# A decoder block with routed experts: stage borders without GpSimd's drain, routing's last rounds a step ahead, expert rows and weights waited for apart, and bfloat16 pad and rank matrices

## The chip, the cores and the metric

The kernel runs on one core of one Trainium2 chip. The time is that of the device for one execution, in microseconds (us). Engines: TensorE (PE, matrix products; PEld is its weight load), VectorE (DVE), ScalarE (ACT), GpSimd (POOL), and SyncE (SP), which issues transfers.

## What is computed

The input x has 16 items of 256 tokens by 256 channels, in float32. Two decoder layers follow each other; these are the reference's last lines, with the routed experts' core:

```python
x = x + _L0_attn_ref(_layernorm(x), ...)      # 16 heads, |i - j| <= 32
x = x + _L0_xattn_ref(ctx, ctx, _layernorm(x), mask_BxS2, ...)   # 77 keys, padded
x = x + _L0_ffn_ref(_layernorm(x), ...)       # 8 experts, top 2
x = x + _L1_attn_ref(_layernorm(x), ...)      # causal
x = x + _L1_xattn_ref(_layernorm(x), ctx, ctx, mask_SxS2, ...)
x = x + _L1_ffn_ref(_layernorm(x), ...)       # gated, 4 bit weights, quantised

# _L0_ffn_ref
gate_weights = softmax(x @ gate_w + gate_b)
topk_vals, topk_idx = top_k(gate_weights, 2)
h = gelu(x @ w1[e] + b1[e]); h = gelu(h @ w2[e] + b2[e])
expert_out = h @ w3[e] + b3[e]
sum(topk_vals * take_along_axis(expert_out, topk_idx))
```

## The kernel before

The program runs in four parts, each an `nc.Block` in which every engine has its own instruction stream and the engines meet by semaphores: stage 1 of attention (window, then cross with padding, and at its end the routing of layer 0's experts), the experts, stage 2 of attention (causal, then cross with a mask), and the quantised last network. x stays in on-chip memory.

`attention()` serves both stages. It is a software pipeline over N = 32 units (16 items through self-attention, then 16 through cross-attention). `step(t, ref)` on each engine does lag 0 of unit `ref`, lag 1 of the one before and so on, in eight parts i = 0 to 7. In stage 1 lag 4 is the layer norm of the finished item, lag 5 its turning (`last_turn`, `keep_turned`), lag 6 the gate logits (`gate_logits`, `see`, `find_best`, `choose`; GpSimd's `note` keeps them), and lag 7 the ranks: `ranks` on TensorE counts with a triangular matrix `row_before`, a matrix of ones, the choices `both` and the counts `filled`, which place in its expert's region each token gets; `place` turns it into a slot; `scatter` on GpSimd casts the slots, adds to `filled`, and sends the item's rows to `slots_dram` by four indirect transfers. The last item comes to lag 7 at step N + 6. Then `tile_table` makes the table of tiles from `filled`, and SyncE writes zeros behind each expert's last row (L563), waits for them, and ends.

In the cross part `scores` adds the pad bias as a product of a selecting matrix and the padding row `pad_now` (L1301), ahead of the heads' products (L1308).

`experts()` goes over MT = 71 tiles of 128 rows, each belonging to one expert, with a ring of four buffers. SyncE loads per tile its rows (L1640, 128 KB) and the expert's packed weights (L1642, 2180 KB) when y of the tile four before is made. TensorE's order in tile j is: turn the rows of tile j + 1 (`turn_rows`, L1671), layer 2 of tile j (L1696, 32 matmuls), layer 1 of j + 1 (L1680, 16), layer 3 of j (L1706). VectorE copies the turned rows (`columns`, L1743) and adds y's bias (L1754); ScalarE does the gelus (L1724); GpSimd stores y (L1657). Aside from that, VectorE quantises the raw weights of the last network (`beside`: at tiles 0, 2, 3 and the last seven, behind the y addition), which SyncE has loaded right after tile 0 (L1648, three of 768 KB); at the end TensorE turns them in twelve runs through two PSUM buffers and ScalarE copies them out (L1737).

A part ends at its `nc.Block` line (L458 for both attention stages, L1632 for the experts, L1951 for the last network), where each engine executes a drain and then passes a barrier. Then the context manager `semaphores` clears the part's semaphores on GpSimd (L49) and has all engines pass a second barrier (L50).

## Time and profile before

| What | Value |
|---|---|
| Median of 3 runs | 2347.57 us (2342.65 to 2357.03) |
| Profiled execution | 2332.47 us, its span 2330.9 us |
| Mean granted TensorE clock | 0.949 |
| Busy share PE, DVE, ACT, POOL | 90%, 53%, 41%, 29% |
| Stage 1, experts, stage 2, last network end at | 735.5, 1294.8, 1994.9, 2330.9 us |
| Memory rate in the experts | about 341 GB/s, transfer engines over 90% busy |

All times within the program are from that one profiled execution, counted from the start of its span. A row of the timeline is: start, duration (or the busy sum of a merged group of x instructions), engine, line, operation, output<-inputs, shapes, and in brackets the idle time of the engine before it and what ended that. A q behind an engine's name means its queue: drains, waits and issues. 1.00 of the granted clock is 2.4 GHz and 0.50 is 1.2 GHz.

### The profile page before, as it was taken

How to read it: one execution, taken by the hardware profiler on the slowest of the kernel's cores; microseconds unless marked ns; L12 is line 12 of the kernel's file. 1: busy time of each engine (PE TensorE's matmuls, PEld its weight loads, DVE VectorE, ACT ScalarE, POOL GpSimd, SP SyncE). 2: the span in 40 equal slices, each digit the busy share in tenths (PEclk: the TensorE clock that was granted, in tenths of full speed). 3: DMA queues.
4: the chain of work that ended last, by engine and by line, in shares of the span. 5: the costliest groups of instructions: out<-in, count | busy, mean ns of one | idle time of the engine just before them, and what ended most of it. 6: DMA issues, size and time to landing. Idle time of an engine off the chain costs nothing. (4 is left out here: it accounts for less than half of the span.)

```text
span 2330.9 us, 50427 instructions
## 1 busy us (share of the span) xinstructions
PE 2109.1 (90%) x16962; PEld 1618.0 (69%) x16962; DVE 1228.9 (53%) x5368; ACT 962.8 (41%) x1843; POOL 675.6 (29%) x1222
## 2 busy tenths in 40 slices
PE   5999999999992999999999589999999999799869
PEld 3777777777762899999999367677766666344358
DVE  4677775555532211111113467777767776439964
ACT  1444454555541233333333235455554454237510
POOL 2555555244443000000000434544321121003410
PEclk8899999998975999999999789999999999899989
DMA  6223222222314899999996533333223222000013
GB/s 203 88 95 108 104 100 95 82 93 92 101 58 175 311 342 341 340 343 341 342 342 257 158 102 121 118 110 112 92 79 95 95 89 66 5 0 0 0 47 98
DMA packets 209352, 334.56 MB, mean 144 GB/s; under 512 B 59445, under 2 KB 193498, under 8 KB 200122
## 3 DMA queue, kind: packets, MB, share of 16 engines
q1 hardware_dynamic: 195306, 302.46, 37.1%
q0 software_dynamic: 9552, 26.10, 3.8%
q10 hardware_dynamic: 4352, 4.20, 0.5%
q8 instruction: 78, 1.28, 0.2%
q14 instruction: 64, 0.52, 0.1%
HBM read 193.72 MB, written 28.05 MB: 95 GB/s over the span
## 5 line engine op out<-in xcount | busy, mean ns | idle before, releaser
L1724 ACT ACTIVATE moe_h<-moe_h_ps,moe_weights 128x128 f32<-128x128 f32 x568 | 177.3, 363 | 368.4 <-PE moe_h_ps L1696 311.4
L1696 PE MATMUL moe_h_ps<-moe_h,moe_weights 128*128 128x128 f32 x2272 | 267.5, 276 | 0.0
L1754 DVE TENSOR_TENSOR moe_y<-moe_y_ps,moe_weights 128x256 f32<-128x256 f32 x71 | 30.2, 425 | 442.1 <-PE moe_y_ps L1706 442.1
L1696 PEld LDWEIGHTS moe_h_ps<-moe_h,moe_weights 128*128 128x128 f32 x2272 | 261.7, 193 | 0.1
L1125 ACT ACTIVATE causal_prob<-causal_ps 128x768 f32<-128x768 f32 (+1 forms) x192 | 168.6, 878 | 150.8 <-PE causal_ps L1344 149.7
L2148 PE MATMUL ffn_prod_ps<-x_sb,ffn_weights 128*128 128x512 f32 x480 | 210.5, 598 | 9.7 <-ACT ffn_sig_q L2134 7.0
L867 DVE CUSTOM_DVE_ANT_0 causal_masked<-causal_ps,causal_causal_mask 128x256 bf16<-128x256 f32 (+1 forms) x512 | 152.2, 354 | 75.4 <-PE causal_ps L1308 74.5
L1657 POOL DMA_DIRECT2D moe_y_dram<-moe_y x71 | 38.9, 547 | 519.9 <-DVE moe_y L1754 519.9
L2148 PEld LDWEIGHTS ffn_prod_ps<-x_sb,ffn_weights 128*128 128x128 f32 x480 | 90.9, 191 | 127.0 <-issue 110.0
L867 DVE CUSTOM_DVE_ANT_0 window_masked<-window_ps,window_window_mask 128x160 bf16<-128x160 f32 x512 | 135.1, 320 | 76.3 <-PE window_ps L1308 75.5
L1680 PE MATMUL moe_h_ps<-moe_rowsT,moe_weights 128*128 128x128 f32 x1136 | 140.7, 278 | 5.1 <-DVE moe_rowsT L1743 5.1
L1680 PEld LDWEIGHTS moe_h_ps<-moe_rowsT,moe_weights 128*128 128x128 f32 x1136 | 134.2, 194 | 6.3 <-DVE moe_rowsT L1743 6.3
L1706 PE MATMUL moe_y_ps<-moe_weights,moe_h 128*128 128x256 f32 x568 | 134.5, 380 | 0.7 <-ACT moe_h L1724 0.7
L1125 ACT ACTIVATE window_prob<-window_ps 128x640 f32<-128x640 f32 x128 | 89.9, 702 | 108.8 <-PE window_ps L1344 107.7
L721 POOL TENSOR_SCALAR_AFFINE_SELECT causal_prob<-causal_prob 128x512 f32<-128x512 f32 x128 | 80.2, 650 | 167.4 <-ACT causal_prob L1125 167.3
L1308 PEld LDWEIGHTS causal_ps<-k_pair,q_pair 64*128 64x128 f32 x1024 | 73.0, 188 | 67.9 <-issue 44.8
L1308 PE MATMUL window_ps<-k_pair,q_pair 64*128 64x160 f32 (+1 forms) x1024 | 96.5, 290 | 22.7 <-DVE window_m_tok L867 14.9
L1308 PEld LDWEIGHTS window_ps<-k_pair,q_pair 64*128 64x128 f32 x1024 | 78.3, 195 | 55.8 <-DVE window_m_tok L867 24.3
L1308 PE MATMUL causal_ps<-k_pair,q_pair 64*128 64x78 f32 (+2 forms) x1024 | 99.4, 296 | 19.3 <-DVE causal_m_tok L867 15.2
L2005 DVE TENSOR_REDUCE ffn_peak<-ffn_wide 128x1 f32<-128x1024 f32 x72 | 87.2, 1212 | 49.3 <-ACT ffn_wide L2108 49.3
L867 DVE CUSTOM_DVE_ANT_0 causal_masked<-causal_ps,causal_cross_mask 128x77 bf16<-128x77 f32 x512 | 86.7, 236 | 49.1 <-PE causal_ps L1308 49.1
L1706 PEld LDWEIGHTS moe_y_ps<-moe_weights,moe_h 128*128 128x128 f32 x568 | 102.5, 190 | 11.9 <-ACT moe_h L1724 0.9
(352 smaller groups left out, 4497.0 us busy)
## 6 DMA issues: line engine op xcount, KB each, us to landing
moe_weights<-moe_w_in SPq DMA_DIRECT2D x71, 2180.0 KB, 9.6
q_pair<-window_q_parts SPq DMA_DIRECT2D x256, 128.0 KB
q_pair<-causal_q_parts SPq DMA_DIRECT2D x256, 128.0 KB
k_pair<-window_k_parts SPq DMA_DIRECT2D x128, 128.0 KB
k_pair<-causal_k_parts SPq DMA_DIRECT2D x128, 128.0 KB
moe_rows<-moe_slots_dram SPq DMA_DIRECT2D x71, 128.0 KB, 3.5
moe_y_dram<-moe_y POOLq DMA_DIRECT2D x71, 128.0 KB, 3.7
k_pair<-window_k_parts SPq DMA_DIRECT2D x128, 38.5 KB
```

The lines of the kernel that those rows point to most:

```text
L721: op = nc.gpsimd.affine_select(out=m, in_=m, compare_op=ALU.is_ge, fill=0.0, base=0, pattern=[[0, 4], [1, P]], channel_multiplier=-1)
L867: op = nc.vector.tensor_tensor_reduce(masked[:, junk, 0:nk_real], ps1[:, ab, p * L.width1 + col:p * L.width1 + col + nk_real], L.mask_nat[ ...
L1125: nc.scalar.activation(out, src, ACT.Exp).then_inc(expd, 1)
L1308: op = nc.tensor.matmul(ps1[:, ab, j * L.width1 + col:j * L.width1 + col + nk], q_pair[par][rows_of[ab], i + j, qt * P:qt * P + P], k_pair ...
L1657: pool.dma_start(route.y_dram[bass.ds(j * TM, TM), :].rearrange("(s p) d -> p s d", p=P), y[r][:])\
L1680: op = nc.tensor.matmul(h1_ps[:, f // 2, (f % 2) * TM:(f % 2) * TM + TM], w1[:, k, f * P:f * P + P], rowsT[:, k, :], start=(k == 0), stop= ...
L1696: op = nc.tensor.matmul(h2_ps[:, f // 2, (f % 2) * TM:(f % 2) * TM + TM], w2[:, k, f * P:f * P + P], h1[:, k, :], start=(k == 0), stop=(k ...
L1706: op = nc.tensor.matmul(y_ps[:, r % YR, s * D:s * D + D], h2[:, k, s * P:s * P + P], w3[:, k, :], start=(k == 0), stop=(k == FB - 1))
L1724: nc.scalar.activation(out[:, f, :], psum[:, f // 2, (f % 2) * TM:(f % 2) * TM + TM], ACT.Gelu, bias=bias[:, f:f + 1]).then_inc(done, 1)
L1754: nc.vector.tensor_tensor(y[r][:], y_ps[:, r % YR, 0:TS * D].rearrange("p (s d) -> p s d", s=TS), b3.unsqueeze(1).to_broadcast([P, TS, D]) ...
L2005: return nc.vector.tensor_reduce(out, rows, AX.XY, ALU.max, apply_absolute_value=True)
L2148: op = nc.tensor.matmul(prod_ps[:, slot, f, :].rearrange("p (b t) -> p b t", b=2), w[:, k, at:at + P], x_cols(n // GROUPS, k), start=(k == ...
```

## The change

- *Borders.* The blocks of `attention` and `experts` are opened with `no_gpsimd_drain=True`, so that GpSimd meets the barrier without a drain. `semaphores` is no context manager any more: parts end without clearing and without the second barrier. Stage 1's semaphores are cleared on GpSimd at the head of the experts, all others at the program's end, with one barrier there. The setup blocks and the last network's block keep GpSimd's drain.
- *Routing.* `scatter` is split into `count` (casts and additions to `filled`) and `scatter` (the four transfers). The rounds that were done at the steps from N + 3 on are done one step earlier (`ahead`), at i = 7: on TensorE ahead of the last item's output projection, on ScalarE behind the last layer norm's application, on GpSimd as count, note, scatter. The stage has one step fewer (N + 6). The semaphores of routing are taken only by the stage that routes.
- *Experts.* Rows and weights have semaphores of their own: `turn_rows` waits for the rows, `layer1` for the weights. The raw weights' loads stand behind tile 3's loads. `beside` stands between `columns` and the wait for layer 3, in the last seven tiles only. VectorE copies out every other of the twelve turned runs.
- *bfloat16.* `row_before`, `both`, `pad_rows`, `pad_now`, the pad's selecting matrix (now `to_all`) and a new matrix of ones `ones_b` are bfloat16; their entries are 0, 1 or the pad's value. Two of the three rank products and all pad products become bfloat16; the one with `filled` stays float32.

```diff
-    yield sem
-    nc.clear_and_free_semaphores(taken)
-    nc.all_engine_barrier()
+    return sem, taken
...
             gate_b = sb("gate_b", [P, NE], F32)
-            row_before = sb("row_before", [P, P], F32)
+            row_before = sb("row_before", [P, P], BF16)
+            ones_b = sb("ones_b", [P, P], BF16)
             iota_e = sb("iota_e", [P, NE], F32)
...
                 L.padT_u8 = sb("padT_u8", [S2, B], U8)
-                L.pad_rows = sb("pad_rows", [P, B, S2P], F32R)
+                L.pad_rows = sb("pad_rows", [P, B, S2P], BF16)
                 L.padT = sb("padT", [S2, B], F32)
-                L.pad_now = [sb(f"pad_now{i}", [P, S2P], F32R) for i in range(2)]
+                L.pad_now = [sb(f"pad_now{i}", [P, S2P], BF16) for i in range(2)]
...
+        def inline(ref, lag):
+            return routing(ref, lag) and ref < N + 3
+        def ahead(ref, lag):
+            return ref >= N + 2 and routing(ref + 1, lag)
         def ring(ref, lag):
...
-        with nc.Block() as block:
+        with nc.Block(no_gpsimd_drain=True) as block:
             @block.sync
...
                     nc.gpsimd.tensor_tensor(route.filled[:], route.filled[:], both[par][:, 1], ALU.add).then_inc(counted, 1)
+                def scatter(t, ref):
+                    e, r = tail_item(t, 7), ring(ref, 7)
                     pool.wait_ge(slots_cast, 2 * e + 2)
...
                           .then_inc(pad_ready, 1)
-                    if routing(ref, 7):
+                    if inline(ref, 7):
+                        count(t, ref)
                         scatter(t, ref)
...
                                               v_stage[0:kr, 0:kt * H]).then_inc(v_in, 1)
-                    if routing(ref, 6):
+                    if inline(ref, 6):
                         note(t, ref)
+                    if ahead(ref, 7):
+                        count(t + 1, ref + 1)
+                    if ahead(ref, 6):
+                        note(t + 1, ref + 1)
+                    if ahead(ref, 7):
+                        scatter(t + 1, ref + 1)
...
                             split_max(t, ref, 1, 0)
-                        if i == 4 and routing(ref, 7):
+                        if i == 4 and inline(ref, 7):
                             place(t, ref)
-                        if i == 5 and routing(ref, 6):
+                        if i == 5 and inline(ref, 6):
                             find_best(t, ref)
-                        if i == 7 and routing(ref, 6):
+                        if i == 7 and inline(ref, 6):
                             choose(t, ref)
+                        if i == 7 and ahead(ref, 7):
+                            place(t + 1, ref + 1)
+                        if i == 7 and ahead(ref, 6):
+                            find_best(t + 1, ref + 1)
+                            choose(t + 1, ref + 1)
                         if i >= 4 and in_merge(ref, 2):
...
                             apply_norm(t, ref)
+                        if i == 7 and (ahead(ref, 6) or ahead(ref, 7)):
+                            see(t + 1, ref + 1)
                     if ref == 0:
...
                             nc.tensor.matmul(ps1[:, ab, 0:L.pairs * L.width1].rearrange("p (j k) -> p j k", k=S2P),
-                                             selects[rows_of[ab], 4, :], rows, start=True, stop=False,
+                                             to_all[rows_of[ab], :], rows, start=True, stop=False,
                                              skip_group_check=True)
...
                                      skip_group_check=True)
-                    nc.tensor.matmul(out[:, NE:2 * NE], route.ones[:], both[par][:, 0], start=False, stop=True,
+                    nc.tensor.matmul(out[:, NE:2 * NE], ones_b[:], both[par][:, 0], start=False, stop=True,
                                      skip_group_check=True).then_inc(rank_mm, 1)
...
                             if route:
-                                wait(pe, seen, tail_item(t, 6))
+                                wait(pe, seen, tail_item(t, 6) + (0 if ref < N + 3 else 1))
                             last_turn(t, ref, 0)
-                        if i == 2 and routing(ref, 6):
-                            if not in_tail(ref, 5):
-                                pe.wait_ge(last_ev, 2 * B)
-                                pe.wait_ge(seen, tail_item(t, 6))
+                        if i == 2 and inline(ref, 6):
                             gate_logits(t, ref)
-                        if i == 2 and routing(ref, 7):
-                            if not routing(ref, 6):
-                                pe.wait_ge(seen, B)
+                        if i == 2 and inline(ref, 7):
                             ranks(t, ref)
+                        if i == 7 and ahead(ref, 6):
+                            wait(pe, oT_ev, N)
+                            pe.wait_ge(seen, tail_item(t + 1, 6))
+                            gate_logits(t + 1, ref + 1)
+                        if i == 7 and ahead(ref, 7):
+                            pe.wait_ge(seen, tail_item(t + 1, 6))
+                            ranks(t + 1, ref + 1)
                         if i == 2 and active(ref, 0):
...
             y_ps = ipb("y_ps", YR)
+            rows_in = [sem(f"rows_in{i}") for i in range(RING)]
             w_in = [sem(f"w_in{i}") for i in range(RING)]
+            raw_odd = sem("raw_odd")
             turned, copied, l1, act1, l2, act2, l3, y_done = (
...
-            with nc.Block() as block:
+            with nc.Block(no_gpsimd_drain=True) as block:
                 @block.sync
...
                         sp.dma_start(rows[r][:], route.slots_dram[bass.ds(at, TM), :].rearrange("(s p) d -> p s d", p=P))\
-                          .then_inc(w_in[r], 16)
+                          .then_inc(rows_in[r], 16)
                         sp.dma_start(weights[r][:], a["moe_w"][bass.ds(e, 1)].squeeze(0)).then_inc(w_in[r], 16)
                     def load_raw(j):
-                        if j:
+                        if j != RING - 1:
                             return
...
+                    nc.clear_and_free_semaphores(stale)
                     tiles(pool, tile)
...
-                        pe.wait_ge(w_in[r], uses * 32 + 32)
+                        pe.wait_ge(rows_in[r], uses * 16 + 16)
                         for k in range(KC):
...
-                    def layer1(j, r):
+                    def layer1(j, r, uses):
                         w1 = views(weights[r])[0]
+                        pe.wait_ge(w_in[r], uses * 16 + 16)
                         pe.wait_ge(copied, j + 1)
...
                         if n >= 2:
-                            pe.wait_ge(raw_kept, n - 1)
+                            pe.wait_ge((raw_kept, raw_odd)[n % 2], n // 2)
                         for q in range(TURN):
...
                     tiles(act, tile)
-                    for n in range(NTURN):
+                    for n in range(0, NTURN, 2):
                         act.wait_ge(raw_turned, n + 1)
-                        nc.scalar.activation(ffn.run(n), raw_ps[n % 2][:, 0:TURN * P], ACT.Copy).then_inc(raw_kept, 1)
+                        nc.scalar.activation(ffn.run(n), raw_ps[0][:, 0:TURN * P], ACT.Copy).then_inc(raw_kept, 1)
...
                             columns(j + 1)
+                        if isinstance(j, int):
+                            beside(j)
                         dve.wait_ge(l3, j + 1)
...
                     def beside(j):
-                        if j == 0:
+                        if j == MT - 7:
                             compact()
                         for m in range(3):
-                            if j == (2, 2, 3)[m]:
+                            if j == (MT - 7, MT - 6, MT - 5)[m]:
                                 find_scales(m)
-                            if j == (3, MT - 7, MT - 7)[m]:
+                            if j == (MT - 6, MT - 5, MT - 4)[m]:
                                 divide(m)
-                            if j == (MT - 6, MT - 6, MT - 5)[m]:
+                            if j == (MT - 4, MT - 4, MT - 3)[m]:
                                 round_off(m)
-                            if j == (MT - 5, MT - 4, MT - 4)[m]:
+                            if j == MT - 3:
                                 clip(m)
-                            if j == (MT - 3, MT - 3, MT - 2)[m]:
+                            if j == (MT - 2, MT - 2, MT - 1)[m]:
                                 rescale(m)
-                    tiles(dve, tile, beside)
+                    tiles(dve, tile)
+                    for n in range(1, NTURN, 2):
+                        dve.wait_ge(raw_turned, n + 1)
+                        nc.vector.tensor_copy(ffn.run(n), raw_ps[1][:, 0:TURN * P]).then_inc(raw_odd, 1)
+        return taken
...
         ffn = FfnWeights(nc, top)
-        layers(nc, a, ident, x_sb, x_flat, ffn, Tail(x_dram.rearrange("(t p) d -> p t d", p=P), x_peak))
-        quantised_ffn(nc, x_sb, ident, ffn, x_peak, x_dram, out_flat)
+        stale = layers(nc, a, ident, x_sb, x_flat, ffn, Tail(x_dram.rearrange("(t p) d -> p t d", p=P), x_peak))
+        stale += quantised_ffn(nc, x_sb, ident, ffn, x_peak, x_dram, out_flat)
+        nc.clear_and_free_semaphores(stale)
+        nc.all_engine_barrier()
```

The order of the instructions at three places. First GpSimd near the end of stage 1, before, around the layer norm of item 15 (`var_eps` to `minus_one`), where the casts, counts, transfers and notes of an item stand as one piece:

```order
L56 TENSOR_TENSOR window_last_var_eps<-window_last_mv,window_last_eps 128x2
L58 TENSOR_TENSOR window_last_rstd<-window_last_var_eps,window_last_half 128x2
L756 TENSOR_TENSOR window_minus_mean<-window_last_mv,window_last_rstd 128x2
L759 TENSOR_TENSOR window_minus_mean<-window_minus_mean,window_minus_one 128x2
L675 CAST window_slot_now<-window_slot_f 128x4
L676 COPY moe_slot<-window_slot_f 128x4
L678 TENSOR_TENSOR moe_filled<-moe_filled,window_both 128x8
L680 TENSOR_TENSOR moe_filled<-moe_filled,window_both 128x8
L685 DMA moe_slots_dram<-ffn_weights,window_slot_now 34688x256 x4
L694 COPY moe_logits<-window_gates 128x16
L695 COPY moe_best<-window_best 128x4
```

The same place after:

```order
L683 CAST window_slot_now<-window_slot_f 128x4
L684 COPY moe_slot<-window_slot_f 128x4
L686 TENSOR_TENSOR moe_filled<-moe_filled,window_both 128x8
L688 TENSOR_TENSOR moe_filled<-moe_filled,window_both 128x8
L706 COPY moe_logits<-window_gates 128x16
L707 COPY moe_best<-window_best 128x4
L697 DMA moe_slots_dram<-ffn_weights,window_slot_now 34688x256 x4
L53 TENSOR_TENSOR window_last_var_eps<-window_last_mv,window_last_eps 128x2
L55 TENSOR_TENSOR window_last_rstd<-window_last_var_eps,window_last_half 128x2
L768 TENSOR_TENSOR window_minus_mean<-window_last_mv,window_last_rstd 128x2
L771 TENSOR_TENSOR window_minus_mean<-window_minus_mean,window_minus_one 128x2
L683 CAST window_slot_now<-window_slot_f 128x4
```

The notes (`moe_logits`, `moe_best`) have moved ahead of the item's four transfers, and item 12's casts, counts and transfers have moved ahead of the layer norm of item 15.

Second, SyncE at the start of the experts, before (rows and weights of a tile, the raw weights, and the next tile's table entries):

```order
L1640 DMA moe_rows<-moe_slots_dram 128x256
L1642 ISA
L1642 DMA moe_weights<-moe_w_in 128x4360
L1648 DMA moe_raw<-L_ffn_w_gate_in 128x6x256
L1648 DMA moe_raw<-L_ffn_w_up_in 128x6x256
L1648 DMA moe_raw<-L_ffn_w_down_in 128x2x768
L1638 TENSOR_LOAD moe_tile_expert
L1638 ISA x2
L1639 TENSOR_LOAD moe_tile_row
L1639 ISA x2
L1640 ISA
L1640 DMA moe_rows<-moe_slots_dram 128x256
```

After, from the weights of tile 2 to the raw weights:

```order
L1674 DMA moe_weights<-moe_w_in 128x4360
L1670 TENSOR_LOAD moe_tile_expert
L1670 ISA x2
L1671 TENSOR_LOAD moe_tile_row
L1671 ISA x2
L1672 ISA
L1672 DMA moe_rows<-moe_slots_dram 128x256
L1674 ISA
L1674 DMA moe_weights<-moe_w_in 128x4360
L1680 DMA moe_raw<-L_ffn_w_gate_in 128x6x256
L1680 DMA moe_raw<-L_ffn_w_up_in 128x6x256
L1680 DMA moe_raw<-L_ffn_w_down_in 128x2x768
```

The three raw loads have moved from behind tile 0 to behind tile 3.

Third, VectorE in the experts, before, at tiles 1 to 3 (`rowsT` is `columns`, `moe_y` the y addition, the others `beside`):

```order
L1754 TENSOR_TENSOR moe_y<-moe_y_ps,moe_weights 128x256
L1743 COPY moe_rowsT<-moe_rows_ps 128x256
L1754 TENSOR_TENSOR moe_y<-moe_y_ps,moe_weights 128x256
L1784 TENSOR_REDUCE moe_wmax<-moe_raw 128x48
L1785 TENSOR_SCALAR moe_wscale<-moe_wmax 128x48
L1786 RECIPROCAL moe_winv<-moe_wscale 128x48
L1784 TENSOR_REDUCE moe_wmax<-moe_raw 128x48
L1785 TENSOR_SCALAR moe_wscale<-moe_wmax 128x48
L1786 RECIPROCAL moe_winv<-moe_wscale 128x48
L1743 COPY moe_rowsT<-moe_rows_ps 128x256
L1754 TENSOR_TENSOR moe_y<-moe_y_ps,moe_weights 128x256
L1789 TENSOR_TENSOR moe_raw<-moe_raw,moe_winv 128x1536
```

After, at the first of the last seven tiles:

```order
L1777 COPY moe_rowsT<-moe_rows_ps 128x256
L1811 TENSOR_TENSOR moe_over<-moe_slot,moe_base 128x448
L1813 TENSOR_TENSOR moe_over<-moe_over,moe_skipped 128x448
L1814 TENSOR_REDUCE moe_shift<-moe_over 128x64
L1815 TENSOR_TENSOR moe_pos<-moe_slot,moe_shift 128x64
L1820 TENSOR_REDUCE moe_wmax<-moe_raw 128x48
L1821 TENSOR_SCALAR moe_wscale<-moe_wmax 128x48
L1822 RECIPROCAL moe_winv<-moe_wscale 128x48
L1790 TENSOR_TENSOR moe_y<-moe_y_ps,moe_weights 128x256
L1777 COPY moe_rowsT<-moe_rows_ps 128x256
L1825 TENSOR_TENSOR moe_raw<-moe_raw,moe_winv 128x1536
L1820 TENSOR_REDUCE moe_wmax<-moe_raw 128x48
```

The side work has left the first tiles, and stands behind `columns` of the next tile and ahead of the y addition, where it stood behind the y addition and ahead of `columns`.

## Rows read from the trace of the kernel before

**Rows 1.** Windows: us, busy time (instructions) by engine, clock, DMA share, GB/s

```profile
480.00:650.00 170.00, 166.26 (x1481) 121.91 (x1482) 91.95 (x356) 89.08 (x165) 79.43 (x179) 0.93 0.31 100
...
740.00:760.00 20.00, 4.78 (x20) 4.09 (x21) 0.42 (x1) 1.25 (x4) 0.00 (x0) 0.50 1.00 390
```

**Rows 2.** Y additions in order of time; the middle row groups 61 of them

```profile
769.67 0.42 DVE L1754 TENSOR_TENSOR moe_y<-moe_y_ps,moe_weights 128x256 f32<-128x256 f32 x1 [8.83 <-PE moe_y_ps L1706]
...
L1754 DVE TENSOR_TENSOR moe_y<-moe_y_ps,moe_weights x61: 424/425/426, 803.1 to 1241.5; 128x256 f32<-128x256 f32 x61
...
1285.86 0.42 DVE L1754 TENSOR_TENSOR moe_y<-moe_y_ps,moe_weights 128x256 f32<-128x256 f32 x1 [4.19 <-PE moe_y_ps L1706]
```

**Rows 3.** L458, end of both attention stages: min/median/max ns, first and last start

```profile
L458 ACTq DRAIN  x2: 394/492/591, 729.5 to 1991.9; - x2
L458 POOLq DRAIN  x2: 5291/5666/6040, 730.1 to 1988.7; - x2
...
L458 SPq DRAIN  x2: 7/65/123, 735.0 to 1987.2; - x2
```

**Rows 4.** Instructions of L1632, the end of the experts

```profile
L1632 POOLq DRAIN  x1: 5860/5860/5860, 1288.9 to 1288.9; - x1
...
L1632 ACTq DRAIN  x1: 519/519/519, 1292.2 to 1292.2; - x1
```

**Rows 5.** The program's first border: a drain of L2239, and what starts next

```profile
L2239 DVEq DRAIN  x1: 596/596/596, 5.5 to 5.5; - x1
...
6.35 0.10 POOL L570 MEMSET window_eps<- 128x2 f32 x1 [2.05 <-POOLq L2239]
```

**Rows 6.** First instructions of stage 2 and of the last stage, timeline

```profile
1295.57 0.10 POOL L570 MEMSET causal_eps<- 128x2 f32 x1 [8.45 <-POOLq L50]
...
1996.06 0.19 POOL L1965 MEMSET ffn_ones_rows<- 2x128 f32 x1 [6.59 <-POOLq L50]
```

**Rows 7.** Start of the experts, timeline: start us, us, engine, line, operation

```profile
738.58 0.35 SPq L1642 DMA_DIRECT2D moe_weights<-moe_w_in  x1
...
747.29 0.69 PE L1671 MATMUL moe_rows_ps<-ident,moe_rows 128*128 128x128 f32 x2 [23.63 <-DMA moe_weights<-moe_w_in]
...
748.49 3.78 PE L1680 MATMUL moe_h_ps<-moe_rowsT,moe_weights 128*128 128x128 f32 x16 [0.52 <-DVE moe_rowsT L1743]
...
752.31 0.62 ACT L1724 ACTIVATE moe_h<-moe_h_ps,moe_weights 128x128 f32<-128x128 f32 x2 [1.08 <-PE moe_h_ps L1680]
...
759.69 0.69 PE L1671 MATMUL moe_rows_ps<-ident,moe_rows 128*128 128x128 f32 x2 [7.41 <-DMA moe_weights<-moe_w_in]
...
760.17 5.95 PE L1696 MATMUL moe_h_ps<-moe_h,moe_weights 128*128 128x128 f32 x32
```

**Rows 8.** Tiles 2 to 4 of the experts, timeline

```profile
784.63 1.74 DVE L1784 TENSOR_REDUCE moe_wmax<-moe_raw 128x48 f32<-128x1536 f32 x1
...
790.09 2.05 PE L1680 MATMUL moe_h_ps<-moe_rowsT,moe_weights 128*128 128x128 f32 x16 [2.05 <-DVE moe_rowsT L1743]
```

**Rows 9.** TensorE in the cross part of stage 1, timeline

```profile
560.61 0.41 PE L1301 MATMUL window_ps<-window_pad_now,selects 64*128 64x312 f32 x2
560.86 0.53 PE L1308 MATMUL window_ps<-k_pair,q_pair 64*128 64x78 f32 x8
...
562.91 0.37 PE L1399 MATMUL window_misc<-window_both,window_row_before 128*128 128x16 f32 x2
563.13 0.37 PE L1401 MATMUL window_misc<-moe_filled,moe_ones 128*128 128x16 f32 x2
```

**Rows 10.** Routing's last rounds on GpSimd, timeline

```profile
702.06 0.19 POOL L759 TENSOR_TENSOR window_minus_mean<-window_minus_mean,window_minus_one 128x2 f32<-128x2 f32 x1
...
704.39 1.06 POOL L685 DMA_INDIRECT moe_slots_dram<-ffn_weights,window_slot_now  x1 [0.56 <-issue]
...
722.81 0.20 POOL L680 TENSOR_TENSOR moe_filled<-moe_filled,window_both 128x8 f32<-128x8 f32 x1
```

86 lines of the change are left out of this document (45 added, 41 removed).

## The prediction

> **What bounds the kernel now.** I read the granted clock and the busy time by window first, then the y additions as a ruler of the experts' pace, then the lines that end a stage, and last the experts' start in order of time. In the second half of stage 1 TensorE is busy 166.26 of 170.00 us, at a granted clock of 0.93 [rows 1]: that stretch is TensorE's. In the experts a y addition comes every (1241.5 − 803.1) / 60 = 7.31 us and waits for TensorE [rows 2]; only the first and the last tiles leave that pace. Between stages nothing computes: the reader is to see in [rows 3] that one drain, GpSimd's, lasts long after the others. So the change can gain where engines wait, at three borders and the experts' ramp and tail, and by less work on TensorE.
>
> **Borders.** A stage ends when the last engine has drained. GpSimd's drain takes 5.29 or 6.04 us, ScalarE's 0.39 or 0.59 [rows 3]; in the experts 5.86 against 0.52 [rows 4]. Without it the border is passed when the next latest engine is through. What a passing costs then stands at the program's first border: VectorE's drain starts at 5.5 and takes 0.60, the next instruction starts at 6.35, 0.25 later [rows 5]. That border has no second barrier; the three changed ones lose theirs.
> - Experts to stage 2: ScalarE's drain ends at 1292.2 + 0.5 = 1292.7, so 1292.97 against 1295.57 [rows 4, 6]: 2.6 us.
> - Stage 2 to the last stage: ScalarE's drain starts at 1991.9 and ends at 1992.3 to 1992.5, so 1992.55 to 1992.75 against 1996.06 [rows 3, 6]: 3.3 to 3.5, 3.4 taken.
> - Stage 1 to experts: GpSimd drains from 730.1 to 735.4, but SyncE's own drain runs from 735.0 to 735.1 (it waits for the spare rows' stores) [rows 3], so of the drain only 0.3 us goes. From the end of GpSimd's drain to the first instruction the other two borders take 1295.57 − 1294.8 = 0.8 and 1996.06 − 1994.7 = 1.3 us where 0.25 would do; so 0.3 + 0.55 to 1.05, 1.2 taken. The clearing moves to the head of GpSimd's queue in the experts, whose first own work there is the y store behind 769.67: hidden. Without that cover it is paid as now.
>
> Sum 7.2 us. Low end 4.0, if each border has one more short drain and step of the barrier (1.1 us) to go through.
>
> **Experts' start.** Now TensorE turns a tile's rows only when rows and weights have landed. W0 is issued at 738.58; the turning starts at 747.29, layer 1 at 748.49 [rows 7]. With the rows waited for alone, turning and copy lie ahead of W0's landing, and layer 1 starts at 747.29: 1.2 us. The last gelu of tile 0's layer 1 ends at 752.31 + 0.62 = 752.93, but TensorE, which has the turning of tile 1's rows queued ahead of tile 0's layer 2, stands 7.41 us until W1 lands, and layer 2 starts at 760.17 [rows 7]. With rows apart layer 2 follows the gelu by some 0.1: 7.1 us more. What is late next is layer 1 of tile 1, which now waits for W1. W1 landed 21.1 us after W0's issue, behind two tiles and the raw loads, 3 × 2.36 = 7.1 MB: 0.335 MB/us. Without the raw loads ahead it lands after 4.7 / 0.335 = 14.1 us, at 752.7; layer 2 of tile 0 ends 5.95 us after 753.0, so W1 is not late. y of tile 0 comes 8.3 us earlier. The clock adds to it: layer 1's 16 matmuls take 3.78 us here and 2.05 later [rows 7, 8], so this is the lower level (0.50 in [rows 1]); with no 7-us hole between them it may rise earlier: 0 to 2.2, 0.9 taken. Sum 9.2 us.
>
> The raw loads now stand behind W3. W4 waits for y of tile 0 (the ring has four buffers) and queues behind 5 × 2.36 MB; with its own 2.36 that is 14.2 MB, 42.3 us at 0.335. Layer 1 of tile 4 is wanted some 3 us ahead of y of tile 3, (769.67 − 8.3 − 738.58) + 3 × 7.31 − 3 = 41.7 us after the first issue: a stall of 0 to 1.5 us, 0 taken, since the 21.1 us include the transfers' first delay.
>
> **VectorE's side work.** At tiles 2 and 3 it stands ahead of the copy of the next tile's rows: layer 1 of tile 4 starts at 790.09, after 2.05 us idle on that copy [rows 8]. From y of tile 0 to y of tile 4 there are 803.1 − 769.67 = 33.4 us, where four paces make 29.2: 4.2 us [rows 2]. The change puts all of it into the last seven tiles, between the copy and the wait for layer 3. There VectorE is free for 7.31 less two operations of 0.42; a tile's portion is at most two to three operations over 128 × 1536, 1.74 us each [rows 8], so it fits, and 4.2 is gained. At the end six additions take 1285.86 − 1241.5 = 44.4 us [rows 2] against 6 × 7.31 = 43.9, and the last tile has no successor's layer 1 beside it (up to 2.05): 0.5 to 2.6, 1.5 taken.
>
> The twelve final copies lie between 1286.3 and ScalarE's drain at 1292.2, 0.49 us each. Two engines could save half, 3.0 us. But TensorE refills a buffer only when its copy is out, two buffers in turn; the loop of a buffer stays, and VectorE's copy is no shorter: −0.3 taken (−0.5 to 3.0).
>
> TensorE gets 71 more waits, on semaphores long up; no row shows one alone. As an instruction each is worth no more than one of the 16 matmuls in 2.05 us, 0.13: 0 to 9 us. 0 is taken, since they stand in the queue beside a wait that is there now.
>
> **bfloat16.** The pad bias goes in by 64 pairs of matmuls of 312 columns. A pair takes 560.86 − 560.61 = 0.25 us, 0.40 ns a column [rows 9]: one column a cycle of 2.4 GHz. So bfloat16 can save their weight loads at most: 0 to 5 us, 1.5 taken. The ranks are three pairs of f32 matmuls in 16 rounds, 563.13 − 562.91 = 0.22 us a pair [rows 9]; two of the three become bfloat16. 32 × 0.22 = 7.0 is the upper bound, 0 the lower, half taken: 3.5. Sum 5.0, on the path since TensorE is 98% busy.
>
> The Trainium skill (TensorE: Matmul & The Clock Gate, section Weight-path perf modes — Fast Weight Load (FWL) and DoubleRow) has it that 128 weights of a type that isn't fp32 load about twice as fast. Were the pad pairs bound by their weights, that would save half, 8 us instead of 1.5, and the sum would come to 2315 us; the column rate of the row speaks against it, and no row here shows such a load.
>
> **Routing's last rounds.** Rounds and notes move one step ahead on GpSimd, notes in front of the four scatters. The stage's end hangs on count 15, last row at 722.81 [rows 10]: from 704.39 on GpSimd's own queue is the chain, 18.4 us for three items' counts and scatters, and the change leaves every instruction of it there. It can start earlier by the last projection, which stood ahead of item 12's ranks on TensorE: 8 × 256 columns, as many as layer 1's 16 × 128, 3.8 us at that clock [rows 7]. But the layer norm of item 15, over at 702.06 + 0.19 now, then stands behind item 12's scatters (4 × 1.06 us and gaps, some 5) and ends near 707.1; ScalarE's normalising follows, then `see` and `place`, so scatter 13 comes later than now by 0.5 to 1 us. Bounds 1.5 lost and 1.3 gained; −0.9 taken.
>
> **The sum.** 7.2 + 9.2 + 4.2 + 1.5 − 0.3 + 5.0 − 0.9 = 25.9 us. The profiled execution took 2332.5 us (span 2330.9), so 2306.6. The runs' median, 2347.57, is 1.0065 times its time; in its terms 2321 us.
>
> **Rivals.**
> - *The clock in stage 1 becomes whole.* At 0.93 the stretch lost 0.07 × 170 = 12 us. Gain 38: 2309 us. For: the mean over the run is 0.949, so most stretches have it higher; against: nothing here takes a wait from TensorE there. Chance 0.12.
> - *The drain is only moved.* GpSimd's 5 to 6 us may be work that its next instruction waits for: the gathers of stage 2, the constants of the last stage. Borders two and three give nothing: gain 20, 2327 us. For: nothing else shown explains so long a drain; against: its queue was out of work before it. Chance 0.12.
> - *The ramp is the transfers'.* 390 GB/s [rows 1] may be all there is, and rows that come back late behind W0 leave the 7.1 us: gain 19, 2328 us. Chance 0.10.
> - *Slower than before.* The lower clock level takes more of the stretch at 0.93, because TensorE's work between its waits on VectorE got shorter. It decides from a mean of 0.93 × 170 / (170 + 26) = 0.81 down; at 0.76 it loses 170 × (0.93 / 0.76 − 1) = 38 us, 12 more than is gained: 2360 us. For: the clock was already below 1 there, and 0.50 in the window where TensorE is busy 4.78 of 20 us; against: it stays over 95% busy [rows 1]. Chance 0.05. The Trainium skill (same page, section What's actually happening) calls the throttled state the default, released by activity; the rows agree in direction (1.2 GHz in that window).
> - *The forecast*: 0.61, its own range 2314 to 2329.
>
> **Range and chances.** Low ends (4.0, 6, 3, 0.5, −0.5, 1, −1.5: 12.5) give 2335, high ends (7.5, 10.5, 4.2, 2.6, 3.0, 9, 1.3: 38) 2309; the first rival with half of its own spread below goes to some 2303. Range 2303 to 2337. A change within 1% can't be told from none; 1% faster is below 2324. The forecast has 0.46 of its 0.61 there, the first rival 0.12: faster 0.58, same 0.38, slower 0.04.
>
> **What would show it.** Right: 0.3 us from the last short drain to the first instruction; y of tile 4 within 29.3 us of y of tile 0; a pad pair hardly below 0.25 us; no idle time of TensorE on W1. Wrong: gathers that start late behind a border; TensorE idle on W1 or W4; a window of stage 1 below 0.9.

## The result and the profile after

| | Kernel before | Changed kernel |
|---|---|---|
| Median of the runs beside each other | 2348.37 us (2342.65 to 2357.03) | 2318.0 us (2309.55 to 2322.45) |
| Ratio, 95% interval | | 0.985 (0.982 to 0.987) |
| Profiled execution | 2332.47 us | 2322.45 us |
| Mean granted clock of it | 0.949 | 0.957 |
| Count 15 (GpSimd's addition to `filled` for item 15, the end of stage 1's chain) starts at | 722.8 us | 730.5 us |
| W0 (the weights of tile 0) issued, behind count 15 by | 15.8 us | 14.3 us |
| W0 issued to the last y addition | 547.3 us | 530.9 us |
| Last y addition to the first instruction of stage 2 | 9.7 us | 7.6 us |
| GpSimd's first instruction of stage 2 to its first of the last network | 700.5 us | 702.2 us |

The forecast was 2321 us; the runs say 2318. The two profiled executions are only 10 us apart, the medians 30 (the ratio, taken of 2348, makes 35); the profiled execution of the kernel before, at 2332.47, lies below all four runs of its median. Two things are to be explained: where the borders' and the experts' terms went in the profile, and why stage 1 looks 8 us longer in it.

The granted clock of the changed kernel over the program, in 40 slices:

```profile
PEclk8999999999875999999999799999999999999989
```

The windows of [rows 1], of the changed kernel (us; busy time and instructions of TensorE, its weight loads, VectorE, ScalarE, GpSimd; clock, DMA share, GB/s):

```profile
480.00:650.00 170.00, 149.85 (x1357) 107.89 (x1355) 86.51 (x334) 83.81 (x156) 73.89 (x170) 0.92 0.29 92
740.00:760.00 20.00, 7.12 (x40) 6.32 (x41) 0.85 (x2) 2.67 (x6) 0.00 (x0) 0.56 0.78 306
```

Drains and first instructions behind them, where [rows 3], [rows 4] and [rows 6] stood before (L465 ends both attention stages, L1664 the experts):

```profile
L465 ACTq DRAIN  x2: 399/494/589, 737.2 to 1984.5; - x2
...
L465 SPq DRAIN  x2: 7/66/124, 742.7 to 1979.9; - x2
```

```profile
L1664 ACTq DRAIN  x1: 519/519/519, 1281.8 to 1281.8; - x1
...
L1664 DVEq DRAIN  x1: 592/592/592, 1282.5 to 1282.5; - x1
```

```profile
1283.35 0.10 POOL L577 MEMSET causal_eps<- 128x2 f32 x1 [6.30 <-POOLq L1664]
```

```profile
1985.24 0.17 DVE L2047 TENSOR_REDUCE ffn_top<-x_peak 128x1 f32<-128x16 f32 x1 [1.41 <-PEq L465]
1985.51 0.20 POOL L2005 MEMSET ffn_ones_rows<- 2x128 f32 x1 [3.42 <-POOLq L465]
```

The start of the experts by time, and the y additions (answering to [rows 7] and [rows 2]):

```profile
744.87 0.35 SPq L1674 DMA_DIRECT2D moe_weights<-moe_w_in  x1
...
746.53 0.69 PE L1704 MATMUL moe_rows_ps<-ident,moe_rows 128*128 128x128 f32 x2 [15.14 <-DMA moe_rows<-moe_slots_dram]
...
753.27 3.78 PE L1714 MATMUL moe_h_ps<-moe_rowsT,moe_weights 128*128 128x128 f32 x16 [6.06 <-DMA moe_weights<-moe_w_in]
...
757.77 3.84 PE L1730 MATMUL moe_h_ps<-moe_h,moe_weights 128*128 128x128 f32 x32 [0.29 <-ACT moe_h L1758]
...
761.45 1.95 PE L1714 MATMUL moe_h_ps<-moe_rowsT,moe_weights 128*128 128x128 f32 x16
```

```profile
765.16 0.42 DVE L1790 TENSOR_TENSOR moe_y<-moe_y_ps,moe_weights 128x256 f32<-128x256 f32 x1 [7.22 <-PE moe_y_ps L1740]
```

```profile
L1790 DVE TENSOR_TENSOR moe_y<-moe_y_ps,moe_weights x61: 423/424/426, 794.6 to 1233.0; 128x256 f32<-128x256 f32 x61
```

```profile
1275.79 0.42 DVE L1790 TENSOR_TENSOR moe_y<-moe_y_ps,moe_weights 128x256 f32<-128x256 f32 x1 [4.19 <-PE moe_y_ps L1740]
```

A border now takes 0.3 us behind its last drain (VectorE's at the end of the experts: 1282.5 + 0.6 = 1283.1, first instruction 1283.35). y of tile 0 comes 20.3 us after W0's issue, where it took 31.1; the 61 additions in the middle keep their pace, (1233.0 − 794.6) / 60 = 7.31. Layer 2 of tile 0 starts 4.5 us after layer 1 and runs its 32 matmuls in 3.84 us instead of 5.95.

### The profile page after: what moved, and what is told of

It reads as the page before. It is cut to its first block and busy times, and to the rows that moved or that the text cites. A ratio compares the mean times of both kernels' runs of the same rounds, so it can differ in the third digit from the quotient of the medians.

```text
span 2320.8 us, 50344 instructions
## 1 busy us (share of the span) xinstructions
PE 2089.0 (90%) x16930; PEld 1598.4 (69%) x16930; DVE 1231.0 (53%) x5374; ACT 960.7 (41%) x1837; POOL 677.3 (29%) x1223
## 5 line engine op out<-in xcount | busy, mean ns | idle before, releaser
L1334 PE MATMUL window_ps<-k_pair,q_pair 64*128 64x160 f32 (+1 forms) x1024 | 103.3, 305 | 23.1 <-DVE window_m_tok L886 14.9
L1334 PEld LDWEIGHTS causal_ps<-k_pair,q_pair 64*128 64x128 f32 x1024 | 73.0, 188 | 72.4 <-issue 42.1
L1334 PE MATMUL causal_ps<-k_pair,q_pair 64*128 64x78 f32 (+2 forms) x1024 | 99.4, 296 | 23.7 <-DVE causal_m_tok L886 19.3
L1334 PEld LDWEIGHTS window_ps<-k_pair,q_pair 64*128 64x128 f32 x1024 | 77.7, 196 | 55.9 <-DVE window_m_tok L886 24.6
```

Of the source, the lines that this page charges most:

```text
L1334: op = nc.tensor.matmul(ps1[:, ab, j * L.width1 + col:j * L.width1 + col + nk], q_pair[par][rows_of[ab], i + j, qt * P:qt * P + P], k_pair ...
```

## The experiments

All ratios are to the kernel before, run beside the kernel on the same chip. The runs came in three groups, one after the other and each on a chip of its own: u_f32, u_noahead, b_borders and b_experts (chip 7); x_again, n_again, n_f32 and h_late (chip 2); x_third, h_next, p_pads and e_rawfirst (chip 15). What differs between groups may thus come from the chip or from the time of the run; no run tells these apart. The changed kernel itself ran in the second and third group, and in the comparison above, but not in the first. Terms within the program are read between two instructions of one trace, so that the rest of the trace does not enter. A *hole* below is time in which TensorE stands still ahead of the output projection of a step with routing, since ScalarE's copy of the turned output comes late; the lines of one are shown further down.

### The borders alone

The kernel before with:

```diff
-        with nc.Block() as block:
+        with nc.Block(no_gpsimd_drain=True) as block:
-    yield sem
-    nc.clear_and_free_semaphores(taken)
-    nc.all_engine_barrier()
+    return sem, taken
```

in attention and experts, the clearing at the head of the experts and at the program's end, and the semaphores of routing taken by stage 1 alone.

> The kernel before with the borders' part alone: no GpSimd drain in attention and experts, no clearing and second barrier at their ends. My sum: 7.2 us less, ratio 0.9969; first instructions 0.3 us behind the last short drain. Rival (the drain is only moved to GpSimd's next work): 1 to 2 us less, ratio 0.9995, and the gathers of stage 2 or the constants of the last stage start 4 to 6 us late.

Measured: 0.9965 (0.9949 to 0.998), 8 us. Its trace at the end of the experts, with the last drain, the first instruction and the first gather of stage 2:

```profile
L1632 ACTq DRAIN  x1: 519/519/519, 1302.2 to 1302.2; - x1
```

```profile
1302.98 0.10 POOL L568 MEMSET causal_eps<- 128x2 f32 x1 [5.92 <-POOLq L1632]
...
1304.38 1.04 POOL L664 DMA_INDIRECT causal_got<-moe_y_dram,causal_got_pos  x1 [0.90 <-POOL causal_got_pos L658]
```

1302.2 + 0.5 = 1302.7, first instruction 0.3 later. The gather follows the first instruction by 1.4 us, as it does in the changed kernel and in the kernel before. So GpSimd's next work does not wait for what its drain waited for: the second rival falls.

### The experts' part alone

The kernel before with the semaphores `rows_in` and `w_in` apart, the raw loads behind tile 3's, `beside` in the last seven tiles, and the copies on two engines:

```diff
-                        pe.wait_ge(w_in[r], uses * 32 + 32)
+                        pe.wait_ge(rows_in[r], uses * 16 + 16)
...
+                        pe.wait_ge(w_in[r], uses * 16 + 16)
                         pe.wait_ge(copied, j + 1)
...
-                        if j:
+                        if j != RING - 1:
                             return
```

> The kernel before with the experts' part alone (rows and weights apart, raw loads behind tile 3, VectorE's side work in the last seven tiles, copies on two engines). My sum: 9.2 + 4.2 + 1.5 - 0.3 = 14.6 us less, ratio 0.9938, five y additions within 29.3 us from the first one. Rival (the ramp is bound by the transfers): W0 lands later, 7 us of it gone, ratio 0.9967.

Measured: 0.9936 (0.9921 to 0.9951), 15 us. In its trace y of tile 0 comes 20.0 us after W0's issue (31.1 before), y of tile 4 another 29.9 later (33.5 before, 29.3 expected), and the last y 531.1 after it (547.3).

### The raw loads back behind tile 0

The changed kernel with:

```diff
-                        if j != RING - 1:
+                        if j:
```

> The changed kernel with the raw loads back behind tile 0's. By my sum W1 then lands 7 us later (2.36 MB at 0.335 MB/us) and layer 1 of tile 1 waits for it, but layer 2 of tile 0 does not: TensorE idles some 2 to 3 us on W1 in layer 1 and y of tile 0 comes 2 to 3 us later than in the changed kernel, ratio 0.986. If the transfers bound the ramp anyway, no change.

Measured: 0.9807 (0.9792 to 0.9822), beside 0.9795 (0.9778 to 0.9813) of the changed kernel in the same group: 3 us or so, within both intervals; the trace tells it better. y of tile 0 comes 24.5 us after W0's issue, 4.4 us later than with the raw loads behind tile 3 (20.1 in the same group's trace). It is neither W1 nor layer 1 that waits:

```profile
724.71 0.44 PE L1704 MATMUL moe_rows_ps<-ident,moe_rows 128*128 128x128 f32 x2 [2.97 <-DMA moe_rows<-moe_slots_dram]
...
724.98 5.36 PE L1730 MATMUL moe_h_ps<-moe_h,moe_weights 128*128 128x128 f32 x32
```

The turning of tile 1's rows waits 2.97 us for those rows, and layer 2 of tile 0, queued behind it, starts 2.6 us behind the gelu and mostly at the low clock (5.36 us against 3.84). SyncE spends 5.05 us on issuing the last raw load (710.83), so even the small transfer of rows is late: it is issued at 717.19, 7.8 us behind W0, where it is 1.7 in the same group's changed kernel (709.57 and 707.90). Of the 10.8 us that the ramp gained, 4.4 are thus the raw loads' place and the other 6.4 the waits set apart.

### bfloat16 undone

The changed kernel with `row_before`, `both`, `ones_b` in float32 and `pad_rows`, `pad_now`, `to_all` in fp32r, the types that they or their forerunners had in the kernel before:

```diff
-            row_before = sb("row_before", [P, P], BF16)
+            row_before = sb("row_before", [P, P], F32)
...
-                L.pad_rows = sb("pad_rows", [P, B, S2P], BF16)
+                L.pad_rows = sb("pad_rows", [P, B, S2P], F32R)
```

> The changed kernel with the pad and rank matrices in their old types (fp32r and float32). Theory A (bfloat16 only saves time on TensorE, 5 us): 5 us slower than the changed kernel, ratio to the kernel before 0.987, and in its trace the last transposes of each routed item (L1557) still end 1.7 to 2.5 us late from 505 us on, since these holes have another cause. Theory B (the holes that the changed kernel has in front of the projection, about 2.2 us in nine steps, and the falls of the clock behind them come from the bfloat16 matmuls): the holes are gone and the time is about 10 us lower than the changed kernel's.

Measured: 0.9906 (0.9892 to 0.992), where the changed kernel had 0.985 in its own comparison: 12 us, not 5, but not side by side. Theory A has the direction and half of the size. Theory B falls: the holes are there with float32 too, 1.1 to 2.1 us at six steps and 0.3 at a seventh. Within this group the partner with bfloat16 is u_noahead (below), at 0.9799: 25 us, with the place of the last rounds mixed in.

### Only the ranks back in float32

```diff
-            row_before = sb("row_before", [P, P], BF16)
-            ones_b = sb("ones_b", [P, P], BF16)
+            row_before = sb("row_before", [P, P], F32)
+            ones_b = sb("ones_b", [P, P], F32)
...
-            both = [sb(f"both{i}", [P, ST, NE], BF16) for i in range(2)]
+            both = [sb(f"both{i}", [P, ST, NE], F32) for i in range(2)]
```

> The changed kernel with the rank matrices back in float32, the pads in bfloat16. By my sum bfloat16 ranks are worth 3.5 us and pads 1.5: ratio 0.9865. If the pads carry most of it (the distance from one pad pair's start to what follows the scores fell by 0.1 us, 64 pairs make 6.4 us), the ratio is within 2 us of the changed kernel's, 0.9855.

Measured: 0.9863 (0.9845 to 0.9881) beside 0.9795 for the changed kernel in its group: the ranks alone are worth 0.7%, 16 us. The pads don't carry most of it. That the ratio is the one of my sum, 0.9865, is chance: the sum went with 0.985 for the changed kernel, which had 0.9795 here. What they do is to be seen in TensorE's timeline, first with float32 ranks:

```profile
552.67 0.37 PE L1425 MATMUL window_misc<-window_both,window_row_before 128*128 128x16 f32 x2
552.89 0.37 PE L1427 MATMUL window_misc<-moe_filled,moe_ones 128*128 128x16 f32 x2
553.12 0.37 PE L1430 MATMUL window_misc<-window_both,window_ones_b 128*128 128x8 f32 x2
553.34 1.09 PE L1510 MATMUL window_misc<-window_cross_pad_ctx_b,window_cross_pad_wk 128*128 128x77 f32 x8
...
555.17 1.10 PE L1334 MATMUL window_ps<-k_pair,q_pair 64*128 64x78 f32 x8
```

and with bfloat16 ones:

```profile
546.96 0.17 PE L1425 MATMUL window_misc<-window_both,window_row_before 128*128 128x16 bf16 x1
546.98 0.37 PE L1427 MATMUL window_misc<-moe_filled,moe_ones 128*128 128x16 f32 x2
547.20 0.17 PE L1430 MATMUL window_misc<-window_both,window_ones_b 128*128 128x8 bf16 x1
547.23 1.09 PE L1510 MATMUL window_misc<-window_cross_pad_ctx_b,window_cross_pad_wk 128*128 128x77 f32 x8
...
548.86 0.64 PE L1334 MATMUL window_ps<-k_pair,q_pair 64*128 64x78 f32 x8
```

From the first rank product to the next work (the keys' projection, L1510) it takes 553.34 − 552.67 = 0.67 us against 0.27. The saving is 0.40 us in a step, not the 0.22 that I put down. The steps tell how much of this is TensorE's time alone: those wholly at the full clock take 18.4 us in the kernel before, 18.1 in p_pads and 17.7 in the changed kernel. So the bfloat16 pads save 0.3 us a step and the ranks 0.4, 11 us together in 16 steps; the ranks' 6 leave some 10 of their 16 us to the clock. The second thing is behind it: in the float32 trace the products that follow slow down (the 8 score products of L1334 take 1.10 us instead of 0.64), and in the bfloat16 trace they don't. The windows of the two traces:

```profile
480.00:650.00 170.00, 164.99 (x1496) 119.25 (x1496) 93.84 (x361) 90.77 (x165) 79.07 (x179) 0.92 0.32 101
```

```profile
480.00:650.00 170.00, 163.22 (x1603) 117.15 (x1601) 99.88 (x389) 98.55 (x179) 86.62 (x198) 0.99 0.32 103
```

TensorE's clock is 0.92 with float32 ranks and 0.99 with bfloat16 ones, with TensorE as busy in both. From count 1 to count 9 the one takes 152.0 us and the other 137.7, 17.7 a step and a shorter last one; its clock falls only 2 us ahead of the end. In the kernel before it took 151.1. In the two traces without holes and with float32 ranks, p_pads and the kernel before, each fall of the clock from 500 to 650 us starts 1 to 2.5 us behind the rank products, in steps of 18 us or more. So the ranks' type changed the clock; why it falls there, with TensorE busy, no run shows. bfloat16 ranks don't keep it up everywhere: in the changed kernel's trace it falls at 634.8, 648.5, 662.1 and 675.8 us, in the last steps of the stage, 0.6 to 2.1 us behind them as well.

### The changed kernel again, twice

> The changed kernel once more, as the partner of the other three on one chip: ratio to the kernel before 0.985. If the holes in front of the projection are a chance of one execution, this trace has them at other steps or of other lengths; if they belong to the program, they stand at the same eight steps from 505 to 656 us.

> The changed kernel a third time, as partner on this chip: ratio 0.985, and holes of 1 to 2.5 us at the eight steps between 505 and 656 us.

Measured: 0.9855 (0.9832 to 0.9877) and 0.9795 (0.9778 to 0.9813), the median 2320 and 2280 us; the kernel before beside them 2354 and 2328 us. The trace of x_again has the holes at the eight steps, 0.5 to 3.7 us long. That of x_third has none, so its expectation missed both the ratio and the holes. This is what a hole looks like, in the profile after: ScalarE's copy of the turned output (L1211) waits for four transposes (L1557), and TensorE for the copy:

```profile
566.14 0.66 PE L1557 MATMUL window_misc<-ident,window_o_tok 128*128 128x128 f32 x4
...
568.95 0.60 ACT L1211 ACTIVATE window_oT<-window_misc 128x512 f32<-128x512 f32 x1 [4.95 <-remote]
...
569.60 3.64 PE L1565 MATMUL window_misc<-window_cross_pad_wo,window_oT 128*128 128x256 f32 x8 [2.24 <-issue]
```

and the same without a hole, in x_third:

```profile
554.55 0.66 PE L1557 MATMUL window_misc<-ident,window_o_tok 128*128 128x128 f32 x4
...
555.25 0.60 ACT L1211 ACTIVATE window_oT<-window_misc 128x512 f32<-128x512 f32 x1 [2.84 <-PE window_misc L1557]
...
555.90 2.00 PE L1565 MATMUL window_misc<-window_cross_pad_wo,window_oT 128*128 128x256 f32 x8
```

The copy starts 2.81 us behind the transposes' start instead of 0.70, 0.02 us behind TensorE's semaphore update, which is recorded at 568.93 and 555.23 us: it is the update that is late. The projection follows at the low clock, 3.64 us instead of 2.00 for eight products. So a hole costs 2.1 us and up to 1.6 more of clock. The traces of the first two groups have seven or eight each in the steps with routing (sums of 8 to 15 us; one variant, below, has none), whatever the kernel, and so has the profile after; the third group's four traces have none, and nor has the profiled execution of the kernel before. In those traces count 15 stands at 722.8 us (before), 713.6 (ranks float32) and 693.6 (changed); in traces with holes at 735.4 and 736.1 (stage 1 as before), 730.5 and 716.1 (changed), 708.8 and 721.5 (changed but for the last rounds). The profile of before that I worked from and the profile after are thus of two kinds, and their distance of 10 us is not the change's.

### Routing's last rounds where they were

The changed kernel with `STEPS = N + 7`, all rounds `inline`:

```diff
-            return ref >= N + 2 and routing(ref + 1, lag)
+            return False
```

> The changed kernel with routing's last rounds where they were (N + 7 steps). If the moved rounds cost what I worked out, 0.9 us faster than the changed kernel, and stage 1 ends within 1 us of it, counted from the last item's projection. If the stage's late end in the changed kernel's trace (742.8 against 735.5) comes from the moved rounds, it ends some 7 us earlier. If it comes from the holes of the nine routed steps before, it ends as late, and the holes are there.

> The changed kernel with routing's last rounds back at N + 7 steps, once more: if moving them costs what the first comparison showed (ratios 0.9799 against 0.9849), it is 12 us faster than the changed kernel on this chip; if that was the chip's or the chance's, within 4 us of it; my sum had 1 us.

Measured: 0.9799 (0.978 to 0.9819) the first time, 0.9854 (0.9839 to 0.9869) the second, where the changed kernel had 0.9849 in its own comparison and 0.9855 in the second group. The same program differs by 0.5% between two groups, outside both intervals: an interval holds for its group. Within the second group, side by side, the rounds' place makes no difference (0.9854, 0.9855). In the traces count 9 to count 15 takes 55.6, 56.8, 58.8 and 58.8 us with the rounds ahead (x_again, x_third, the profile after, e_rawfirst) and 56.1 and 56.1 with them in place. u_noahead's trace fits none of its three expectations: the holes are there, but its stage 1 ends much earlier than in the profile after (count 15 at 708.8 against 730.5), and 19 of these 22 us are gained by count 9, ahead of the moved rounds: its holes sum to 9 us against 15.

> The same with the pad and rank matrices in their old types too: the borders' and the experts' part alone. If the parts add up, 0.9965 x 0.9936 = 0.990 of the kernel before, and the distance to n_again is what bfloat16 is worth without the moved rounds: my sum 5 us; if the moved rounds and bfloat16 hinder each other, more than 13 us, the distance of the changed kernel to u_f32 being 10.

This is n_again with the pad and rank matrices in their old types. Measured: 0.9881 (0.9863 to 0.9899), against 0.990 for the two parts multiplied; its distance to n_again is 6 us, the only one of pads and ranks together that was taken within one group and with the same rounds. The changed kernel and u_f32 were 12 apart, u_noahead and u_f32 25. Each has an uncertainty of 5 us or more, and the holes differ from trace to trace; what bfloat16 is worth where there are holes, and whether the moved rounds add to it, stays open.

### The transfers of the slots elsewhere

Two variants without the moved rounds that issue an item's four indirect transfers at other places. Behind the copy of v:

```diff
                     if inline(ref, 7):
                         count(t, ref)
-                        scatter(t, ref)
...
                         note(t, ref)
+                    if inline(ref, 7):
+                        scatter(t, ref)
```

> As n_again, with the four indirect transfers of each item behind the copy of v and the note on GpSimd instead of ahead of them. Theory C (the holes in front of the projection come from the transfers being issued while TensorE turns the normalised output): the holes are gone or stand at another place of the step, and if they are gone the time is some 15 us lower (eight holes of 1 to 2 us, each with a fall of the clock for 3.4 us at half speed behind it). Theory D (something else of the step): holes as in n_again, time within 4 us of it.

Measured: 0.9911 (0.9895 to 0.9928), 14 us slower than its partners, and all eight holes gone: the copy starts 0.31 us behind the start of the last transpose at these steps, in the group in which the partners have 9 to 14 us of holes. The expectation of 15 us less missed what waits for GpSimd at the new place. With the transfers issued at another time, then, no hole comes in this trace. The transfers alone don't make one either: in x_third the second of an item's four is issued at 554.17 us for 0.96 us, over the transposes at 554.55, and the copy isn't late. What TensorE waits for in h_late:

```profile
563.30 0.32 POOL L748 COPY window_cross_pad_ctx_b<-window_cross_pad_ctxT 128x154 f32<-128x154 f32 x1
...
563.76 1.96 PE L1516 MATMUL window_misc<-window_cross_pad_ctx_b,window_cross_pad_wk 128*128 128x77 f32 x8 [1.60 <-issue]
```

The copy of the context (L748) stands behind the transfers on GpSimd, and the keys' projection (L1516) behind that copy; 1.6 us idle each step (2.0 in the first), and the clock in the window 480 to 650 is 0.86, the lowest of all traces.

One step later, between the padding row and the next count:

```diff
+                    if routing(ref, 8) and ref - 1 < N:
+                        scatter(t - 1, ref - 1)
                     if inline(ref, 7):
                         count(t, ref)
-                        scatter(t, ref)
+                        if ref >= N:
+                            scatter(t, ref)
```

> As n_again, but the four indirect transfers of an item are issued one step later, between the copy of the padding row and the next item's count, some 2 us ahead of the place where they were, so that neither the turning of the output nor the copy of the context falls together with them. If the holes come from the transfers being issued while TensorE turns the output, they are gone and nothing else waits: some 15 us less than the changed kernel, ratio 0.979. If the holes follow the transfers wherever they stand, TensorE has them at the step's earlier operations and the ratio is 0.985 or more.

Measured: 0.9801 (0.9783 to 0.9819), the same as the changed kernel beside it, 0.9795. But this was the group in which no kernel has holes, so it says that the other place costs nothing, and not whether it would take the holes away. That is open, and so is what in the chip delays the transposes. No variant that ran beside the changed kernel was faster than it.

## Why the prediction was right, and where it was not

| Step | Forecast | Measured | From |
|---|---|---|---|
| Border 1 | 1.2 us | 1.4 | count 15 to W0: 15.77, 14.33 |
| Border 2 | 2.6 | 2.5 | last y to stage 2: 9.7, 7.2 with the borders alone |
| Border 3 | 3.4 | 3.1 | start of ScalarE's drain to first instruction: 4.2, 1.0 |
| Ramp | 9.2 | 10.8 | W0 to y of tile 0: 31.1, 20.3 |
| Side work, early | 4.2 | 4.0 | y of tile 0 to y of tile 4: 33.4, 29.4 |
| Side work, late | 1.5 | 1.6 | y 64 to y 70: 44.4, 42.8 |
| Copies on two engines | −0.3 | −0.4 | last y to stage 2: 7.2, 7.6 |
| bfloat16, without the clock | 5.0 | 11 | steps at the full clock: 18.4, 17.7, times 16 |
| bfloat16, with it | 5.0 | 6 side by side, 12 and 25 otherwise; 16 for the ranks alone where no holes are | ratios |
| Last rounds | −0.9 | 0, uncertain by some 5 | ratios side by side |

**Borders.** Each step held: the next latest drain passes the barrier 0.3 us later, and nothing on GpSimd is waited for behind it. At the third VectorE's first instruction starts 0.15 us behind the last drain (1984.5 + 0.6 = 1985.1, 1985.24), but GpSimd's, for whose constant TensorE waits, only at 1985.51: the 0.3 us that are missing.

**The ramp.** The mechanism held. Layer 1 starts at W0's landing, 8.4 us behind the issue instead of 9.9 (1.5 gained, 1.2 forecast); layer 2 follows the gelu's end by 0.1 us instead of 7.2 (7.2 gained, 7.1 forecast). What was mis-sized is the clock's part, 0.9 taken of a range to 2.2: layer 2 runs in 3.84 us instead of 5.95, so 2.1. And "what is late next is layer 1 of tile 1" named the wrong thing for the raw loads' old place: with them there the rows of tile 1 come late, not W1. In the forecast's own kernel neither is late: W1 lands at 758.8, 13.9 us behind W0's issue where 14.1 was forecast, and layer 1 of tile 1 starts at 761.45. W4 is barely late: it lands at 783.35 and layer 1 of tile 4 starts at 783.40, so the addition of tile 3 comes 7.44 us behind the one before instead of 7.31; over the traces with the raw loads behind tile 3 it comes 7.3 to 7.9 us behind, a stall of 0 to 0.6 where 0 to 1.5 was put. What the sum left out is the issuing itself: SyncE spends 8.25 and 8.31 us on the last two raw loads, and W4 goes out only at 771.63, 6.5 us behind y of tile 0.

**Copies on two engines.** As forecast, the loop of a buffer stayed: VectorE's copy takes 0.56 us there and ScalarE's 0.49.

**bfloat16.** This step failed in size on both parts. For the pads I argued that a pair at 0.25 us already took a column a cycle, so nothing but weight loads could go. The reading was wrong: the pair's two products, on 64 rows each, start 3 ns apart and run side by side (560.608 and 560.611 in the kernel before), so 0.25 us is 0.79 ns a column, about two cycles, and the row doesn't speak against a saving. In the traces a pair with its scores takes 0.51 us instead of 0.62 (564.82 to 565.33 against 560.61 to 561.22), 64 × 0.11 = 7 us, of which 16 × 0.3 = 5 show in the length of the steps, where I had taken 1.5. By the rule of the Trainium skill (TensorE: Matmul & The Clock Gate, section Weight-path perf modes — Fast Weight Load (FWL) and DoubleRow) my estimate had been 8. The trace agrees with the rule on the load: a pad's weight load takes 92 ns in bfloat16, and took 183. For the ranks I took half of two pairs at 0.22 us; the stretch fell by 0.40 us, 6.4 in 16 rounds and nearly the upper bound of 7.0. The pads' and ranks' direct part is 0.7 us a step: the steps that run wholly at the full clock take 17.7 us, and took 18.4 in the kernel before (606.7 to 625.1).

**The clock, the first rival.** I gave it 0.12 because nothing takes a wait from TensorE there. That was the wrong condition: the clock in stage 1 became nearly whole when the narrow float32 products got shorter, with no wait gone. In the group without holes it did: 0.99 in the window, 2280 against 2328 us, a gain of 48 us, more than the 38 of that rival. In the two traces of the changed kernel with holes the clock falls within 2 us of seven and of five of the eight holes (0.92 and 0.95 in the window), and the gain is 30 to 35. The Trainium skill (same page, section What's actually happening) calls the throttled state the default, released by activity. The falls behind holes, in which TensorE stands still, agree with it. Whether it bears on those behind the narrow products, where TensorE is busy 164.99 of 170.00 us in p_pads, no run here shows. The other-side rival had the sign wrong; shorter work of that kind did not lower the clock.

**The last rounds.** The order of the chain held: the layer norm of item 15 ends behind an item's transfers (it ends at 714.7 in the profile after, the transfers at 713.1), and count 15 hangs on GpSimd's queue. The −0.9 us cannot be told from nothing.

**The number.** By the terms that traces give without holes in them, the borders and the experts bring 23 us where I had 22. Where I had 4, stage 1 brought the rest: 7 to 12 us for the changed kernel with holes (30 to 35 in all; u_noahead, also with holes, has 47 in all), and 29 without (count 15 at 722.8 and 693.6). So the forecast of 2321 us came near 2318 with the right borders and experts, and with a part of stage 1 that was too small by 3 to 8 us. That the range held the first comparison is in part luck. The sum was read from an execution without holes and carried to a median of runs that are slower by the ratio 1.0065, which I took for noise; among runs without holes the same change brings 48 us. In the third group the same change gave 0.9795, which is outside it, if narrowly, when carried to 2347.57 us: 2299.

## What to carry to other kernels

Read terms between two instructions of a trace, not from the ends of the program: all border and experts' terms were within 2 us of the forecast in every group, while the medians of one program differed by almost 2% between groups, which ran on different chips. In a long stretch bound by TensorE, look for float32 products of few columns: they cost more than their columns say (one of 16 columns took 0.22 us to the start of the next, and 0.02 in bfloat16), and the clock may fall behind them. When a drain is long on one engine only, ask who needs what it waits for; here no one did, and each border gave back all that lay beyond the next latest drain.

## What the runs showed of the hardware

- In the groups of runs on chips 7 and 2, and not in that on chip 15, four transposes on TensorE were reported done up to 2.3 us late, mostly 1 to 2 (once 3.7), while GpSimd was issuing indirect transfers, and the granted clock fell for 3.4 to 6.8 us behind most of these holes of the changed kernel. In the one trace of chip 2 with the transfers issued at another time of the step there was no such delay.
- TensorE's clock fell in four of eight steps behind about 1.5 us of float32 products with 8 and 16 columns, and stayed at 2.4 GHz from 500 to 634 us when 0.4 us of these were gone (p_pads and the changed kernel in the third group).
- The weight load of a 64 × 128 matrix took 92 ns in bfloat16 and 183 in fp32r, its product over 312 columns 303 and 411.
- One program's median was 2318 to 2320 us on two occasions and 2280 on a third, on chip 15, with the kernel before at 2348, 2354 and 2328 beside it.
